# Weight blocks of the three layer-0 projections: float32 loads in two halves on SyncE's queue and a cast on ScalarE, in place of one casting load on GpSimd's queue

## The reference, cut to what matters

```python
x = L0_attn_x                                    # (8, 2048, 1024) float32
xn = _layernorm(x, axis=-1)
# inside _L0_attn_ref(xn, Wq, bq, Wk, bk, Wv, bv, Wo, bo):
def proj(W, bias):
    y = jnp.einsum('bte,fe->btf', x, W) + bias   # W is 1024 x 1024 float32
    return y.reshape(b, t, h, dh).transpose(0, 2, 1, 3)
q = _rope(proj(Wq, bq), e)
k = _rope(proj(Wk, bk), e)
v = proj(Wv, bv)
# causal softmax attention over 16 heads, then Wo and bo
s = ...
g = _silu(_L0_ffn_ref(xn, w_gate, w_up, w_down))
x = x + s * g
# layer 1: layernorm, distance attention, mixed linear layer, x + s * g
```

## Time and profile before

| what | us |
|---|---|
| median of 2 runs | 3097.1 (3095.28 to 3098.92) |
| the profiled execution | 3079.2 |
| its span, slowest core (core 2) | 3077.0 |
| spans of the 8 cores | 3058.1 to 3077.0 |
| TensorE busy in matmuls | 2277.7 (74% of the span) |
| VectorE busy | 884.2 (29%) |
| ScalarE busy | 851.3 (28%) |
| GpSimd busy | 78.3 (3%) |
| mean granted TensorE clock of core 2 | 0.780 |

### The profile page before, as it was taken

The page is one execution under the profiler, slowest core; times in us unless marked ns, Lnnn a source line. Parts: engine busy times, 40 slices in busy tenths (PEclk is TensorE's granted clock), DMA queues, the critical chain, the costliest instruction groups (busy, mean ns, idle before and its releaser), DMA issues.

```text
span 3077.0 us, 39771 instructions; the slowest of 8 cores (3058.1 to 3077.0 us)
## 1 busy us (share of the span) xinstructions
PE 2277.7 (74%) x15153; PEld 1250.5 (41%) x15302; DVE 884.2 (29%) x1695; ACT 851.3 (28%) x1191; POOL 78.3 (3%) x148
## 2 busy tenths in 40 slices
PE   3799999984676646797776777529777687787887
PEld 1344444432233213464664666315457233333332
DVE  4444444431232264433223111240110002202112
ACT  4111111112111145464444444312110233222222
POOL 1011001000000000000000000000000000000000
PEclk8899999997878865656556555659899998888877
DMA  6122222102111010101001000243225102001010
GB/s 164 20 33 33 33 31 35 28 1 58 17 18 17 1 28 29 63 2 62 2 2 57 8 1 2 92 148 97 70 80 179 28 0 55 29 26 55 4 52 28
DMA packets 58555, 129.71 MB, mean 42 GB/s; under 512 B 7673, under 2 KB 15867, under 8 KB 55812
## 3 DMA queue, kind: packets, MB, share of 16 engines
q1 hardware_dynamic: 34052, 92.56, 9.0%
q0 software_dynamic: 24320, 34.61, 7.4%
HBM read 142.88 MB, written 18.88 MB: 53 GB/s over the span
## 4 chain that ended last, share of the span: by engine, by line
PE 57%; ACT 15%; DVE 13%; issue 8%; DMA 5%; DVEq 0%; ACTq 0%; SPq 0%; POOL 0%; PEldq 0%; POOLq 0%
PE PS L912 8%; ACT EB L934 7%; PE PS L746 7%; PE PS L618 5%; PE PS L1222 5%; PE PS L627 5%; PE PS L1385 5%; PE PS L1454 4%; PE PS L661 4%; PE PS L1190 3%; DVE PS L917 2%; ACT PRJ L754 2%; PE PS L1311 2%; DVE ACC L672 2%; PE PS L978 1%
## 5 line engine op out<-in xcount | busy, mean ns | idle before, releaser
L912 PE MATMUL PS<-Q,K 64*128 64x128 bf16 x2176 | 274.2, 305 | 123.5 <-ACT EB L934 118.4
L934 ACT ACTIVATE EB<-PS,negBh 128x1152 bf16<-128x1152 f32 (+7 forms) x128 | 204.1, 1594 | 256.5 <-DVE PS L917 242.7
L912 PEld LDWEIGHTS PS<-Q,K 64*128 64x128 bf16 x2176 | 211.7, 135 | 153.1 <-issue 142.4
L661 PE MATMUL PS<-HT,WDT 128*128 128x512 bf16 x745 | 188.7, 389 | 39.1 <-DVE HT L644 21.9
L746 PE MATMUL PS<-XN,WBLK 128*128 128x512 bf16 x746 | 206.0, 440 | 12.8 <-DVE K L761 5.1
L1222 PE MATMUL PS<-XN,W1FULL 128*128 128x512 bf16 x747 | 175.0, 388 | 50.8 <-DVEq L95 16.3
L917 DVE TENSOR_TENSOR PS<-PS,trinegT 128x128 f32<-128x128 f32 x256 | 76.6, 300 | 438.7 <-PE PS L912 430.4
L618 PE MATMUL PS<-XN,WGT 128*128 128x512 bf16 x752 | 170.8, 382 | 27.3 <-DVE XN L443 19.9
L1190 PE MATMUL PS<-identw,PLAND 128*128 128x128 f32 x1024 | 131.4, 293 | 77.3 <-DMA PLAND<-Wsel 67.3
L627 PE MATMUL PS<-XN,WUT 128*128 128x512 bf16 x752 | 168.8, 379 | 0.8
L1385 PE MATMUL PS<-K,Q 128*128 128x512 bf16 x496 | 151.1, 456 | 16.5 <-ACT SCH L1522 8.4
(11 more groups left out here) (165 smaller groups left out, 2505.9 us busy)
## 6 DMA issues: line engine op xcount, KB each, us to landing
PLAND<-Wsel SPq DMA_DIRECT2D x64, 512.0 KB, 4.4
XF<-xT SPq DMA_DIRECT2D x8, 1024.0 KB, 12.3
XT<-xT SPq DMA_DIRECT2D x4, 2048.0 KB, 8.8
x1park<-XT SPq DMA_DIRECT2D x32, 256.0 KB
X1CH<-x1park SPq DMA_DIRECT2D x8, 1024.0 KB, 8.0
XT<-x1park SPq DMA_DIRECT2D x4, 2048.0 KB, 9.7
outT<-XT SPq DMA_DIRECT2D x32, 256.0 KB
LAND<-wu POOLq DMA_DIRECT2D x16, 256.0 KB, 3.7
```

The source lines that it names most:

```text
L661: t.matmul(BK(bki), WDTg[:, dc, ts(hl, 128)], HT[:, hl, ts(n, 512)], start=(hl == 0), stop=(hl == HG - 1)),
L912: tS = P.op("tensor", lambda t, h=h, gi=gi, tt=tt, off=off: t.matmul(PS[:, off + tt * 128:off + (tt + 1) * 128], head_k(h, ts(tt, 128)), h ...
L934: s.activation(EB2[:, slot, 0:klen], PS[:, 0:klen], AF.Exp, bias=negBh[:, h:h + 1]), inc=True)
```

## The change: where the float32 is cast, and who issues the loads

`stage_T` no longer issues a casting load from GpSimd. SyncE issues two plain float32 loads of 128x512 (256 KB each), one for each half of the block, into a new landing buffer FLND with one slot for each half. ScalarE casts each half into the same four landing buffers as before. SyncE waits, before it reloads a half's slot, until ScalarE has cast what is in it, so there is at most one block ahead. TensorE waits for the second cast (`t_land = cvt`) where it waited for the load.

```diff
+    FLND = ar.place("FLND", [128, 2, 512], F32, oW + (36 << 10))
...
+    cvt67 = {0: None, 1: None}
...
         def stage_T(fc):
             li = fc % 4
             sl = fc % 2
-            P.wait("gpsimd", land_guard[li])
-            t_land = P.dma("gpsimd", LANDY(li),
-                           W_d[fc * 128:(fc + 1) * 128, :], sem=f"dl{li}")
+            cvt = None
+            for h in range(2):
+                P.wait("sync", cvt67[h])
+                t_half = P.dma("sync", FLND[:, h, :],
+                               W_d[fc * 128:(fc + 1) * 128,
+                                   h * 512:(h + 1) * 512], sem=f"dp{h}")
+                P.wait("scalar", t_half)
+                P.wait("scalar", land_guard[li])
+                cvt = P.op("scalar", lambda s, li=li, h=h: s.copy(
+                    LANDY(li)[:, h * 512:(h + 1) * 512], FLND[:, h, :]),
+                    inc=True)
+                cvt67[h] = cvt
+            t_land = cvt
             P.wait("tensor", t_land)
             P.wait("tensor", wblk_read[sl])
```

## The result

The changed kernel took 3131.6 us in the median of its runs and the kernel before 3098.9 us beside it. The ratio is 1.011 with a 95% interval of 1.0093 to 1.0127, that is about 34 us more (29 to 39). The forecast was 3126.4 us, 29.3 more, and the range 3109 to 3143. The profiled execution took 3128.1 us, its slowest core (core 5) spans 3126.6 us. In some runs one group of four cores has a lower granted clock than the other; such runs are left out of the ratios.

A forecast was written before the change was run, and what follows sets the result against it. The prediction took the phase as one ring of ScalarE, VectorE and TensorE without overlap; 15.0 + 0 + 3.6 + 0.7 + 2.8 + 7.2 = 29.3 us on 3097.1 gave 3126.4 us, range 3109 to 3143.

The forecast's parts named there:

- Casts behind the product: Blocks 2 to 7 of k and q: two casts after VectorE's product delay TensorE 1.25 us a turn, 15.0 us.
- Casts in v: In the v projection, 3.0 us of cover while TensorE turns V hide 1.25 us of casts: 0.
- Loads: Weight-block loads: 0 for most blocks; +3.6 us at the border k to v, +0.7 at v to q.
- The chain of the second: Border v to q: load, cast and turn of block 1 put its turn at 967.45 instead of 966.63, +0.7 us.
- The rival of late loads: Halves land late every turn of the projections, above some 13 us; slower by over 2%, 3180 us; chance 0.04.
- Start: Start of the phase: block 0's last cast and waiting +0.9, block 1 a load later +1.9; together +2.8 us.
- The clock: Large matmuls of k and q: longer pauses lengthen all 16 blocks to v's length, +7.2 us (-24 to +14).
- So I let all 16 blocks of k and q become as long as v's: 16 x (9.2 - 8.75): Large matmuls in k and q: each block goes from a mean of 8.75 us to 9.2, 7.2 us in all.
- The rule weighed there: TensorE's matmuls: a pause sets the clock back and each following group pays for a new start; fixed price makes +7.2 zero.
- Behind it the barrier and all later work are the same: After the projection phase: barrier and later work unchanged, the attention gains and loses nothing.
- the median of the runs is 17.9 above it: Whole kernel: the median exceeds the profiled execution of 3079.2 us by 17.9, giving 3097.1 us before the change.

The follow-up runs named there:

- the ring kernel: Kernel before, with TensorE in k and q waiting for ScalarE's activations of the block instead of VectorE's product; ratio 0.9828 (0.978 to 0.9876), 53 us less.

## Why the prediction was right, point by point

- **Casts behind the product, +15.0: right in mechanism and size.** Measured 14.0. A cast took 615 ns where the earlier trace rows gave 586 to 630, and a pair 1.14 us. The estimate from the Trainium skill (ScalarE: Activation LUTs, What ACT_TABLE_LOAD costs) was 1.13 us, and the rows agree. The kernel with the casts beside the product takes the cost away, the one with the casts doubled adds it a second time.
- **Casts in v, 0: right.** The pause is 7.73 us in both.
- **Loads, 0 in the middle, +3.6 and +0.7 at the borders: right.** Measured 3.4 and 0.6. (The chain of the second gives 967.45 - 966.63 = 0.82, not 0.7.) Of the first, 2.24 us are ScalarE's wait for the second block's first half. The rival of late loads is out: no cast in the middle of a projection waits for one.
- **Start, +2.8: measured +2.0,** and 2.5 to 3.4 in the later profiles with the tables first. Right in kind. The run with block 0 ahead shows that block 1 waits for the bytes of the tables as long as its own loads are issued behind them.
- **The clock, +7.2: this term was too large; measured +2.6.** The failing step is "So I let all 16 blocks of k and q become as long as v's: 16 x (9.2 - 8.75)". That k and q become as v did come true: 9.00 and 8.96 us against v's 8.97 before. But 9.2 was one block, read to ScalarE's start, and 8.75 a mean of busy times over a stretch. With v's mean from the same rows, 9.0, which the prediction itself works out among its rivals, the term is 16 x 0.25 = 4.0; like for like over eight cores (8.97 against 8.79 and 8.77) it is 3. That there is such a term at all is more than chance: by the median over the cores the blocks of k took 8.79 to 8.91 us in the seven profiles with pauses of 5.88, and 8.95 to 9.01 in three of the four with 7.05 or 7.15 (in the fourth, that with block 0 ahead, most cores had a lower granted clock). The rule weighed there, from the Trainium skill (TensorE: Matmul & The Clock Gate, HAM oscillation), that each group pays for a new start, holds for most blocks here but not for all: on core 2 of the ring kernel the granted clock was 1.00 from 727 to 799 us, with pauses of 3.2 us between the blocks. So it is no fixed price for every pause. The blocks of k (mean over the cores) took 8.1 us with pauses of 3.3, 8.4 with 4.15, 8.8 with 5.88, 9.0 with 7.05 and 8.9 with 8.09: longer with the pause, up to about 7 us, and no further.
- **"Behind it the barrier and all later work are the same": wrong.** The last stage takes about 5 us more in the first pair of profiles and 6 over all of them. With it the sum is 27.7, and with the interval's low end at 29 little is left to explain. The two misses, 4.6 us too much for the clock and 5 to 6 too little for the last stage, went against each other; that the total came within 5 us is in part their doing.
- **"the median of the runs is 17.9 above it": used rightly as an offset,** though its cause was not known then. Most likely it is the mixing stage at the lower clock, which the first execution happened to be spared: the second profile of the kernel before has it on six cores and took 3098.1 us. That is two executions, not a proof.

What stays open: why the last stage is longer with the new loads, and what makes up the 14 to 15 us that the kernel with all casts hidden loses: the start is 3.4 of them and the last stage 1 to 5, so 6 to 11 have no place yet, in an interval that is itself 15 us wide. The only other stage that is longer by more than 2 us in its two profiles is the mixing, which is long in the kernel before too; whether it is long more often with the new loads can't be told from four profiles and ten. No run here took the last stage apart.

## What to carry to other kernels

An instruction on an engine that is idle 70% of the time still costs its full length if it stands behind a wait that also holds the bottleneck: look at where it stands in the engine's list, and move it ahead of the wait before giving up on it. When a ring of three engines sets the time, ask of each wait whether its data are really needed; here one wait taken back to the earlier of two events was worth 53 us (42 of them in the projections), more than anything that the change touched. Average a clock-dependent block time over a stretch and by one definition, before and after, and don't take it from one block.

## What was not expected of the hardware

- The granted clock of some cores, mostly in pairs, falls for one stage (0.70 against 0.89 on the same core, in the same stretch) in some executions and not in others, in both kernels, and this costs such a core some 19 us. One profile of before alone does not show it.
- A longer pause does not always mean a slower block: 8.94 us after 8.1 us of pause, 9.00 after 7.05. In the ring kernel, the blocks of one core (core 2) took 6.95 to 7.17 us seven times in a row, all at a granted clock of 1.00.
- A group of matmuls in unedited code 1.8 ms after the change started at 1.2 GHz on core 5 where it had started at 2.4 GHz before, and the group took 109.1 to 109.5 us on all cores where it had taken 98.8 to 103.4. Changes of a few microseconds in a kernel like this can come from a place that the edit doesn't touch.
